# A fused eight-stage network on one core: the first group of a feed-forward stage normalised in the stage ahead of it, and the mixture's returned rows in another order in DRAM

## What is computed

```python
x = x + _L0_attn_a_ref(_layernorm(x, axis=-1), ...)   # selective scan: stage mamba
x = x + _L0_ffn_ref(_layernorm(x, axis=-1), ...)      # stage ffn1
x = x + _L0_attn_b_ref(_layernorm(x, axis=-1), ...)   # softmax attention: stage attn
x = x + _L0_ffn_ref(_layernorm(x, axis=-1), ...)      # stage ffn2, the same weights
x = x + _L1_attn_a_ref(_layernorm(x, axis=-1), ...)   # stage lin
x = x + _L1_ffn_ref(_layernorm(x, axis=-1), ...)      # mixture of experts: stage moe1
x = x + _L1_attn_b_ref(_layernorm(x, axis=-1), ...)   # stage mix: mixA, mixB, mixC
x = x + _L1_ffn_ref(_layernorm(x, axis=-1), ...)      # stage moe2, the same weights
```

## Time and profile before

| | us |
|---|---|
| median of three runs | 3844.01 |
| the profiled execution's own time | 3838.89 |
| its span on the core | 3837.2 |
| PE busy / DVE busy | 3232.7 (84%) / 2617.3 (68%) |
| ACT busy / POOL busy | 1706.6 (44%) / 1463.7 (38%) |

### The profile page before, as it was taken

One profiled execution on the slowest core, in us unless ns is written; L12 is line 12 of the kernel. 1 busy time (PEld: TensorE's weight loads), 2 busy tenths in 40 slices (PEclk: granted clock), 3 DMA queues, 4 the chain that ended last, 5 costly groups with the idle time before them and its releaser, 6 DMA issues. The chain is left out here.

```text
span 3837.2 us, 55410 instructions
## 1 busy us (share of the span) xinstructions
PE 3232.7 (84%) x15992; PEld 1817.3 (47%) x15993; DVE 2617.3 (68%) x5041; ACT 1706.6 (44%) x3399; POOL 1463.7 (38%) x1547
## 2 busy tenths in 40 slices
PE   7898889888689789797988989786896787998985
PEld 3343334333246543444344356554474476665564
DVE  6999899999967575684857577697345864223435
ACT  5756666666445356365455645212032232223121
POOL 4898889888810121213122100111644100001553
PEclk9999999999989889899898999997998998998997
DMA  4455455455500000000000000620243795000246
GB/s 136 138 140 137 126 138 139 128 133 139 144 1 0 16 1 2 1 2 2 2 2 1 2 1 1 187 69 1 88 139 119 177 139 66 11 16 1 73 131 203
DMA packets 370272, 283.07 MB, mean 74 GB/s; under 512 B 214026, under 2 KB 290366, under 8 KB 370016
## 3 DMA queue, kind: packets, MB, share of 16 engines
q1 hardware_dynamic: 356960, 246.43, 25.5%
q0 software_dynamic: 13056, 33.65, 2.6%
HBM read 205.69 MB, written 76.16 MB: 73 GB/s over the span
## 5 line engine op out<-in xcount | busy, mean ns | idle before, releaser
L608 POOL TENSOR_TENSOR mamba_dBu<-mamba_du,mamba_bcs 128x512 f32<-128x512 f32 x512 | 640.1, 1273 | 123.0 <-DMA mamba_bcs<-mamba_bc 79.5
L531 PE MATMUL mamba_banks<-mamba_hc,ident 128*128 128x512 f32 x1024 | 537.9, 634 | 143.2 <-DVE mamba_hc L847 143.1
L777 ACT ACTIVATE mamba_banks<-mamba_delta,mamba_a_neg 128x512 f32<-128x512 f32 x512 | 352.3, 690 | 182.9 <-DVE mamba_hc L847 172.0
L1542 DVE TENSOR_REDUCE attn_mp<-attn_banks 128x1 f32<-128x512 f32 (+3 forms) x768 | 383.5, 551 | 64.5 <-PE attn_banks L1252 44.1
L531 PEld LDWEIGHTS mamba_banks<-mamba_hc,ident 128*128 128x128 f32 x1024 | 181.6, 196 | 457.1 <-DVE mamba_hc L847 343.0
L847 DVE TENSOR_TENSOR mamba_hc<-mamba_banks,mamba_bcs 128x512 f32<-128x512 f32 x512 | 345.5, 676 | 11.4 <-PE mamba_banks L531 11.4
L840 DVE TENSOR_TENSOR_SCAN mamba_banks<-mamba_banks,mamba_dBu 128x512 f32<-128x512 f32 x256 | 312.1, 1219 | 53.3 <-ACT mamba_banks L777 34.3
L840 DVE TENSOR_TENSOR_SCAN mamba_banks<-mamba_banks,mamba_h_end,mamba_dBu 128x512 f32<-128x512 f32 x256 | 328.6, 1284 | 20.2 <-ACT mamba_banks L777 12.2
L1249 PE MATMUL attn_banks<-attn_kT,attn_qT 96*128 96x512 bf16 (+3 forms) x768 | 269.4, 370 | 12.8 <-ACT attn_kT L1431 5.3
L1264 PE MATMUL attn_banks<-attn_qT,attn_kT 98*128 98x512 bf16 (+3 forms) x768 | 243.8, 337 | 12.4 <-ACT attn_r L1450 4.8
L939 PE MATMUL ffn_hp<-ffn_xT,ffn_w1T 128*128 128x512 f32 x512 | 231.9, 609 | 10.9 <-ACT ffn_xT L160 7.5
(11 more groups left out here) (391 smaller groups left out, 6563.9 us busy)
## 6 DMA issues: line engine op xcount, KB each, us to landing
mamba_bcs<-mamba_bc SPq DMA_DIRECT2D x256, 512.0 KB, 4.8
moe_slots_moe<-moe_pad SPq DMA_DIRECT2D x2, 9252.0 KB, 51.4
moe_xg<-moe_slots_moe SPq DMA_DIRECT2D x144, 128.5 KB, 2.1
mix_qkv<-mixA_qkv SPq DMA_DIRECT2D x8, 1536.0 KB, 5.9
mixA_y<-moe_rows SPq DMA_DIRECT2D x16, 512.0 KB, 6.1
mix_qk<-mix_qkv SPq DMA_DIRECT2D x16, 512.0 KB, 7.4
mix_v<-mix_qkv SPq DMA_DIRECT2D x16, 256.0 KB, 7.5
mix_out<-mixB_oh SPq DMA_DIRECT2D x16, 256.0 KB, 7.5
```

The lines of the kernel that those rows point to most:

```text
L531: pe.matmul(banks[:, SUMS + k % PAIR, :], c.ident[:, :], hc[:, n % RING, :], start=False, stop=True, skip_group_check=True).then_inc(sem(" ...
L608: pool.tensor_tensor(dBu[:, n % RING, :], du[:, v, k, :], bcs[:, i_of(n) % 4, 0, :], ALU.mult)\
L777: act.activation(banks[:, n % RING, :], delta[:, v, k, :], ACT.Exp, scale=a_neg[:, k, st:st + 1])\
L1542: dve.tensor_reduce(mp[:, qt // GT, j, qt % GT, at // 512:at // 512 + 1], banks[:, item % SLOTS, 0:size], AX.X, ALU.max).then_inc(sem("rin ...
```

## The change

There are two parts.

**The first group's rows.** A new class `Ahead` holds the buffers of one normalisation and semaphores of its own, both kept over the four first stages. It has the operations of `Norm.moments`, `power`, `normalise` and `transposes`. mamba's DVE calls `moments` and `normalise` for group 0 ahead of its last two adds, and mamba's POOL calls `power` behind its last two gates; attn does so in its last sequence, ahead of its last adds. The feed-forward stages' PE begins with the transposes of `Ahead`'s rows; their POOL leaves out `power(0)`; their DVE leaves out `moments(0)` and `normalise(0)` and raises six semaphores in their place (`count_first`), so that the counts of the later groups are as before. mamba's own `Norm` uses the same buffers (`shared`).

**The order of the returned rows.** The token of tile t and partition p has row p * 32 + t of `yd`. So the scatter of a tile of tokens goes to rows that are 32 KB apart from partition to partition, and reading a group of 4 tiles back takes from each partition's 32 KB one piece of 4 KB where it took four pieces of 1 KB from four places. In moe2 the second choice's rows go into a view `yr` of the same buffer without the 257th value, so that the destination is in one piece too.

```diff
+class Ahead:
...
+    def moments(self, dve, n, added, count):
+        dve.wait_ge(added, count)
+        if n > 0:
+            dve.wait_ge(self.xn_ready, n * GT)
+        dve.sem_inc(self.x_seen, 1)
+        for j in range(GT):
+            dve.bn_stats(self.st[:, j, :], self.c.x_tile(j)).then_inc(self.stats_ready, 1)
+        dve.wait_ge(self.stats_ready, n * GT + GT)
+        dve.sem_inc(self.stats_seen, 1)
+        for j in range(GT):
+            dve.bn_aggr(self.mv[:, j, :], self.st[:, j, :]).then_inc(self.moments_ready, 1)
...
+    def count_first(self, dve, norm):
+        dve.sem_inc(norm.stats_ready, GT)
+        dve.sem_inc(norm.stats_seen, 1)
+        dve.sem_inc(norm.moments_ready, GT)
+        dve.sem_inc(norm.eps_added, 1)
+        dve.sem_inc(norm.rstd_ready, 1)
+        dve.sem_inc(norm.xn_ready, GT)
...
 # stage_mamba, POOL
                 for k in range(PAIR, CB):
                     gate(G - 1, 1, k)
+                ahead.power(pool, 0)
...
 # stage_mamba, DVE
                 group_loop(dve, group)
+                ahead.moments(dve, 0, sem("out_used"), 2 + START["out_used"])
+                ahead.normalise(dve, 0)
                 for i in range(2):
                     add(G - 1, i)
...
 # stage_ffn, PE, POOL, DVE
-                norm.transposes(pe, 0, first=True)
+                ahead.transposes(pe, use, norm)
                 up(0)
...
-                norm.power(pool, 0)
...
-                norm.moments(dve, 0)
-                norm.normalise(dve, 0, first=True)
+                ahead.count_first(dve, norm)
                 norm.moments(dve, 1)
                 norm.normalise(dve, 1)
...
 # stage_attn, POOL and DVE, in sequence(last=True)
+                    else:
+                        ahead.power(pool, 1)
...
+                    else:
+                        ahead.moments(dve, 1, sem("y_used"), 2 + START["y_used"])
+                        ahead.normalise(dve, 1)
...
 # stage_moe
-                        for t, at in ((xT[:, g * GT * D:(g + 1) * GT * D].rearrange("p (n d) -> p n d", d=D), g * GN),
-                                      (xr[:, g * GT:(g + 1) * GT, 0:D], T + g * GN)):
-                            sp.dma_start(t, yd[at:at + GN, :].rearrange("(n p) d -> p n d", p=P)).then_inc(y_back[g], 16)
+                        for i, t in enumerate((xT[:, g * GT * D:(g + 1) * GT * D].rearrange("p (n d) -> p n d", d=D),
+                                               yr[:, g * GT:(g + 1) * GT, :])):
+                            sp.dma_start(t, yd[i * T:(i + 1) * T, :].rearrange("(p n) d -> p n d", p=P)[:, g * GT:(g + 1) * GT, :])\
+                              .then_inc(y_back[g], 16)
...
 # mix_project
-                        sp.dma_start(y[:, slot, i, :, :], yd[bass.ds(i * T + g * GN, GN), :].rearrange("(n p) d -> p n d", p=P))\
+                        sp.dma_start(y[:, slot, i, :, :], yd[i * T:(i + 1) * T, :].rearrange("(p n) d -> p n d", p=P)[:, bass.ds(g * GT, GT), :])\
...
 # host_constants
-    tokens = np.arange(T, dtype=np.uint32).reshape(TILES, P).T
-    out["moe_ids"] = np.stack([tokens, tokens + np.uint32(T)], axis=1)
+    rows = np.arange(T, dtype=np.uint32).reshape(P, TILES)
+    out["moe_ids"] = np.stack([rows, rows + np.uint32(T)], axis=1)
```

More of the change, by code:

```diff
@@ L360, in stage_mamba @@
     c.prepared["ffn"] = (c.keep_ffn("ffn_w1T", [P, KD, HID]), c.keep_ffn("ffn_w2T", [P, HB, D], BF16), c.keep_ffn("ffn_w2s", [P, 2, D]))
+    ahead = c.prepared["ahead"] = Ahead(c)
     bc = nc.dram_tensor("mamba_bc", (2 * NS, T), F32, kind="Internal").ap()
@@ L907, in stage_ffn @@
     w1T, w2T, w2s = c.prepared["ffn"]
+    ahead, use = c.prepared["ahead"], 0 if name == "ffn1" else 1
     with Local(c, name) as s:
@@ L1102, in stage_attn @@
     nc = c.nc
+    ahead = c.prepared["ahead"]
     with Local(c, "attn") as s:
```

61 lines of the change are left out of this document (49 added, 12 removed).

## The result

| | before | after |
|---|---|---|
| median of five runs, us | 3842.01 (3838.75 to 3846.72) | 3822.23 (3819.37 to 3827.91) |
| the profiled execution, us | 3838.89 | 3822.23 |
| its span, us | 3837.2 | 3820.5 |

(Two more runs of the kernel before were made beside the five of the changed one, so its median isn't the one shown above.) The ratio of the two is 0.995 with a 95% interval from 0.9938 to 0.9961: about 19 us less, 15 to 24 by the interval. The two profiled executions differ by 16.7 us.

A forecast was written before the change was run, and what follows sets the result against it. Bounds: group 0's normalising at feed-forward starts, DMA at launch end, PE in expert loops. Terms −9.7 − 1.7 − 2.4 − 0.3 = −14.1 took the profiled 3838.89 to 3824.8; plus 5.1 for the median, 3829.9 us, range 3824.5 to 3837.

The forecast's parts named there:

- group 0 ahead, at one clock: Start of ffn1 and ffn2: PE's transposes begin when DVE's moments did before, −4.85 and −4.86, in sum −9.7 us.
- the clock in the feed-forward stages: Start of ffn1 and ffn2: a shorter PE pause may keep 2.4 GHz; −1.7 us, ends 0 and −3.4.
- reading back in moe2: End of moe2: 16 loads in pieces of 4 KB run at 389 GB/s in place of 350, −2.4 us.
- reading back in mixA: Start of mixA: only the first load is waited for, 3.0 us at 350 GB/s becomes 2.7 at 389, −0.3 us.
- one of the two keeps its clock, −1.7: ffn1 and ffn2 starts: even odds per stage that the clock stays full, so one stage gains 1.7 us.
- The cap of 1.7 per stage: ffn1 and ffn2: the first square can't come before 1086.1, against 1087.8 by PE, so full clock adds at most 1.7 us.
- Rival A: ffn1 and ffn2: the clock falls in both stages or in none; 3831.6 or 3828.2 us, chance 0.35 in both forms.
- 8.39 MB at 389 take 21.6 us: moe2's loads: time at the rate seen in mixA's start with 3 KB pieces, against 24.0 us at 350 GB/s.
- rival C: Reads in moe2 and mixA: large pieces don't read faster, so −2.4 and −0.3 go; 3832.6 us, chance 0.10.
- rival D: Ends of mamba and attn: the moved work isn't hidden and the adds wait; 3841.3 us, chance 0.05.
- the 0.7 us of the six semaphores: ffn1 and ffn2 starts: DVE raises six semaphores before group 1's moments, taking some 0.7 us.
- rival B: Expert loops: scatters land later than before, PE waits; 3854 us at 2 us longer landing, chance 0.08.

The follow-up runs named there:

- e1: Kernel before with only group 0 normalised ahead, rows of yd in the old order; 3827.88 us against 3839.43, ratio 0.9965.
- e8: e4 plus ACT's copy of group 1's transposes moved earlier and the last group's store cut in three; 3842.05 us against 3868.42, ratio 0.9928.
- e2: Kernel before with only the new order of the rows of yd and its loads; 3838.4 us against 3839.43, ratio 0.9992.
- e7: Changed kernel with 33 rows of yd per partition in place of 32, one unused; loads 412 GB/s, tail behind the last scatter 37.12 us.
- e9: Changed kernel without the second choice's adds at the end of moe2, all loads and stores kept; tail behind the last scatter 37.21 us.
- e4: Changed kernel with idle matmuls filling TensorE's pauses around each feed-forward start; 3815.6 us against 3839.43 for the kernel before, ratio 0.9932.
- e6: Changed kernel with the rows of two tiles together, read back in pieces of 2 KB; loads 389 GB/s, tail behind the last scatter 38.22 us.

## Why the prediction was wrong, and where it was right

The forecast was 7.7 us too high. It splits in three, if the profiled executions are taken as the common measure.

**The base, 5.1 us.** I took the sum in terms of the profiled execution, 3824.8, and added the 5.1 us by which the median of three runs (3844.01) lay above the profiled execution before (3838.89). That was chance. More runs of the kernel before gave medians of 3842.01 (5 runs), 3839.43 (22) and 3841.93 (9), so 2 to 4.6 of the 5.1 us were the median of three; and the profiled execution can lie on either side of a median: for the changed kernel it was the median itself, and in the comparisons below it lay from 3.5 us under it (e1) to 6.9 above (e8). Three runs that spread over 4.7 us don't fix a median to better than some us, and my range gave only 2.7 us for it, on top of the end at full clock. This is the largest part of the miss, but it took the next one too to put the time outside the range: with the base right the forecast is 3824.8, with the terms right 3827.3, and the range moved with either would have held 3822.23. That the terms were too small shows without any base: the forecast difference was 14.1 us, and the interval of the measured one begins at 15.

**The terms, 3.1 us.** The sum was −14.1; the profile shows −17.2 in the places named:

| term | forecast | measured |
|---|---|---|
| group 0 ahead, at one clock | −9.7 | −9.7 (216.08 − 211.24, twice) |
| the clock in the feed-forward stages | −1.7 | −3.3 (−13.0 less −9.7) |
| reading back in moe2 | −2.4 | −3.6 (−3.8 in e2 alone) |
| reading back in mixA | −0.3 | −0.6 |

The step "one of the two keeps its clock, −1.7" failed twice over. In no stage of the profiles of `Ahead` without idle matmuls (twelve stages) did the clock stay full throughout: eight took 213.9 to 214.0, four, all of them ffn1, 212.7 to 212.9. By my own statement of what would show it, the stretch from the transposes to the first square at 1.00 in one of the two stages, the changed kernel's profile says no. In those of e7 and e9 ffn1 did have that stretch at full clock and ffn2 not, and there the clock fell behind the second pause instead:

```profile
1085.97 14.00 PE L1012 MATMUL ffn_hp<-ffn_xT,ffn_w1T 128*128 128x512 f32 x32 [1.16 <-ACT ffn_xT L228]
...
1103.43 15.70 PE L1012 MATMUL ffn_hp<-ffn_xT,ffn_w1T 128*128 128x512 f32 x32 [2.58 <-ACT ffn_xT L228]
```

What made the term larger all the same was not in the forecast: the second pause. Before, a stage lost 3.9 us to two stretches or one long one; now it loses 1.5 to 2.8. In the two profiles the second block went from 15.70 to 14.21 us in both stages, 3.0 of the 3.3 us. The transposes and the first block, which were all that the forecast had priced, gave only the rest: 0.9 + 1.4 us of loss became 1.7 in ffn1, and 0.9 + 1.6 became 2.7 in ffn2. The cap of 1.7 per stage was wrong in its reason, as e4 shows. Rival A had the state (the clock falls in both stages) and the wrong price, 0. Why the clock stays full behind the second pause, the same 2.59 us as before, stays open: of the twelve stages it did so in the ten in which it had fallen in the start, and in the kernel before and e2, where it had fallen in the start too, only in one of four.

"8.39 MB at 389 take 21.6 us" was mis-sized: the rate is 403 to 412, and at 408 it is 20.6 us, −3.4. The 389 of the earlier trace rows isn't that of 3 KB pieces: by the trace's packets, 1.07 MB of that stretch came in pieces of 3 KB and 0.68 MB in pieces of 1 KB. The other row that I read beside it, 385 GB/s from 3824 to 3834, isn't "the old pieces" being loaded with the stores at work, as rival C has it, but the stores by themselves, since the last load has landed by 3825.2.

The Trainium skill (DMA: Bandwidth & Descriptors, section "Why small descriptors are slow (HBM only)") charges about 3 cycles for each packet, from which an estimate is 7% more rate from 1 KB to 4 KB. Measured are 349 at 1 KB, 389 at 2 KB (+11%) and 403 to 412 at 4 KB (+15 to +18%), so the measurement disagrees with it in size. In the traces of these loads a packet of 1 KB took 51 ns on average, one of 2 KB 88 and one of 4 KB 163; a straight line through the three, an estimate, has 37 ns for each KB and some 14 ns for each packet. The rate gained less than this alone would give, for the share of the DMA engines fell from 1.09 to 1.02. No run shows what the 14 ns are.

**The rest, −0.5 us.** The stages that the change leaves alone were 0.5 us longer in sum, each by up to 1.3 either way.

Right were: the hiding of the moved work in both stages (rival D is out; the adds started 2.7 and 2.5 us behind the normalising, where I had forecast 3.9 and 1.3 us of room), the 0.7 us of the six semaphores (0.56: DVE's moments start at 1082.03 behind TensorE's 1081.47), TensorE's pause of about 2 us, the DMA engines as what ends the tail, the scatters (rival B out, landing 2.5 us). Rival C is out by e2 and e6. The Trainium skill's row on large powers of two as row pitch (DMA: Bandwidth & Descriptors, section "Latency and other measured facts") doesn't reach down to 32 KB here: e7 shows no gain from 33.

One sum of the forecast is off: by its own chances D and half of the others make 0.075, and B and the rest 0.105, where it says 0.09 twice. Nothing hangs on it.

## What to carry to other kernels

- A pause of TensorE at a stage's start can cost twice: the pause, and the clock behind it. Here a stage before lost 4.84 us to the one and 3.9 to the other. Look at the granted clock behind every pause of the first tens of us, not only at the one that the change shortens, and price the state of each with a kernel that fills it.
- A comparison of launches whose untouched stages vary by some us can't tell a part of 3 us. Lengths from a fixed row to a fixed row in the profiles did: over the kernels with pieces of 4 KB the tail spread by 0.9 us, and the gain was 3.6 to 4.5. And a forecast for a median should carry the spread of the runs behind that median in its range.
- Rows that are written by an index anyway can be put in the order in which they are read back: here the writes landed in the same 2.5 us, and the reads got 15 to 18% faster.
